# A graph, attention and expert layer on one core: work regrouped on GpSimd and VectorE, gate logits of 20 tiles moved off TensorE, 13 products added in a wait

## The chip, the cores and the metric

The kernel runs on one core of one Trainium2 chip. A core has five engines with a queue of instructions each: TensorE (PE in the profile; matmuls, with the loading of weights shown apart as PEld), VectorE (DVE), ScalarE (ACT), GpSimd (POOL) and SyncE (SP, which here only starts transfers). Engines wait for one another through semaphores alone. The metric is the device time of one execution in microseconds; less is better.

## The reference

Inputs are 3125 nodes with 256 features `x`, 53125 edges (`src`, `dst`, `edge_weight`) and the weights. All is float32. Cut to what matters:

```python
xn = layernorm(x)
# graph part: A is the weighted adjacency, A[src, dst] += edge_weight
h  = A @ xn                                   # 3125 x 256
S0 = softmax((A @ h) @ W0.T + b0)             # 128 wide
S1 = softmax((A @ S0) @ W1.T + b1)            # 128 wide
gnn = tanh([S0, S1] + h)
# attention part, linear: k and v are layer-normed per head of 64
kv  = einsum('bhsd,bhse->bhde', k, v) / S
mix = (q @ kv) @ wo.T + bo
x1 = x + gnn + mix
# expert part: 8 experts, each takes at most C = 489 of its tokens, in order
g = layernorm(x1)
logits = g @ gate_w + gate_b                  # 3125 x 8
idx, prb = argmax and max of softmax(logits)
pos  = running count of earlier tokens with the same idx
y = (relu(g @ w1[idx] + b1[idx]) @ w2[idx] + b2[idx]) * prb   if pos < C else 0
out = x1 + y
```

## The kernel before, in words

The nodes are cut into 25 tiles of 128. Everything on each engine is a list written out by hand; there is no planner. What sets the order is the order of each engine's list and the semaphores between them.

**First stage, a loop over `it`.** The dense adjacency is built in 157 units of up to four 128x128 blocks. In iteration `it` VectorE makes the one-hot matrices of unit `it-2` (`hots`, lines 990 to 999, three 128x512 operations), TensorE multiplies them (`build`, lines 1412 and 1414, unit `it-3`), ScalarE copies the result from PSUM (`evac`, line 706) and stores five units at a time to DRAM, and TensorE multiplies the unit by the layer-normed rows (`apply`, line 1429, unit `it-4`), which sums a strip of four node tiles in PSUM. `hots(u)` waits until `build(u-3)` is done. A strip has 25 units. At its end ScalarE and VectorE each copy one half of the sum to SBUF (`strip_out`; VectorE's at lines 1003 to 1006). TensorE may not start the next strip before both copies are done (semaphores `s_hevA`, `s_hevD`). VectorE's copy stands in the iteration in which it makes the one-hots of the unit five after the strip's last. `hidden_node` then turns the sums, tile by tile, and multiplies them by W0.

For `it` up to 30 the loop also sorts the edges (`spread`, `slot`, `ranks`, `slots`), computes layer norms and the key and value sums. `prepare(g)` unpacks a group of edges; `scales(g)` finishes the layer norm's factors, on which the first rows of ScalarE wait. At iteration 25 VectorE checks whether an edge has found no place (lines 1092 and 1093), and TensorE sums that and the gate weights (lines 1474 and 1475); the flag `rounds` decides on a fallback that these inputs don't take. At iteration 31 `kv_tail` (lines 1028 to 1040) finishes the key/value matrix on VectorE in 26 small operations, each waiting for the one before (`link`). TensorE turns it into the 256x256 matrix `M` at iterations 34 and 36. From iteration 40 every fourth one has a `mix(m)` on TensorE (line 1454), the attention output of tile `m`, which VectorE adds to the rows `X1` (line 1016). GpSimd adds the output bias `bo` to `X1` before that, all 25 tiles one after the other as soon as the layer norms are done (line 583).

**Graph layers.** SyncE loads the adjacency from DRAM in chunks of five units into a ring of five slots (line 515). `strip(l, k)` on TensorE (line 1576) is 25 products of 128x512, each two matmuls in the profile. Other work of TensorE is put in behind given products of a strip by the dictionary `inserts`. The second layer (`l == 1`) has eight strips: five of four tiles (0 to 19), then tiles 20-21, 22-23 and 24. With each goes this chain for the strip before: TensorE `turns` (line 1592), VectorE `biased` (1177, 1179), ScalarE the exponentials, VectorE `summed` (1184, 1186), ScalarE the tanh, VectorE `finished` (1193), `moments` and `root` (layer norm by Newton steps), `normal` (1246), which writes the normed rows `XN`.

**Gate.** TensorE turns the rows of `X1` (`gate_turn`, line 1335), ScalarE copies them (`xtout`, line 777), TensorE multiplies them by the gate weights (`logits`, line 1612, 16 matmuls for four tiles), and VectorE applies the factor and the bias and takes the maximum (`chosen`, lines 1223 to 1242). TensorE counts the tokens of each expert (`counts`), VectorE makes the row numbers (`slotted`), and GpSimd scatters the rows to DRAM by expert. TensorE waits for `counts(k)` of a strip, and so for `chosen(k)`, in the middle of the second strip after it. The loop on VectorE for strip `k` is `chosen(k-2)`, `biased(k-1)` and so on to `root(k-1)`, `slotted(k-2)`, `prob(k-2)`, `normal(k-1)`.

**Experts.** When the last row numbers are there, TensorE waits for the first expert's tokens (loaded back from DRAM), turns them and runs eight experts, `up` (line 1671) and `down` (line 1682).

Of the kernel before, what the change touches and what calls it, by code (L numbers as in the profile page):

```python
# [9 lines left out]
I32 = mybir.dt.int32  # L10
# [4 lines left out]
N = 3125  # L15
# [47 lines left out]
NGT = len(GATES)  # L63
SPLIT = 25
# [33 lines left out]
MIX_AT = {40 + 4 * _m: _m for _m in range(NT)}  # L98
T1_AT, M_AT = 34, 36
# [8 lines left out]
def graph_program(nc, a, out):  # L108
    ctx = ExitStack()
    with ctx:  # L110
# [150 lines left out]
        mv = gate[:, 843:893].rearrange("p (t a) -> p t a", a=2)  # L261
        iota_e = sb("iota_e", [P, NE])
# [21 lines left out]
        TURN = (2, 7)  # L284
        XTB = 3
# [82 lines left out]
        s_gturn = sem("s_gturn")  # L368
        s_xtb = sem("s_xtb")
# [48 lines left out]
        def _(sp):  # L418
# [80 lines left out]
            for l in (0, 1):  # L499
                for q in range(NC):  # L500
# [41 lines left out]
        def _(gp):  # L542
# [35 lines left out]

            gp.wait_ge(s_w, 16 * NWL)
# [5 lines left out]
            gp.wait_ge(s_m, 1)  # L585
            gp.memset(blank, 0.0).then_inc(s_blank, 1)
            gp.wait_ge(s_blank, 1)
            gp.memset(blank[:, ROW - 1:ROW].bitcast(I32), NOWHERE).then_inc(s_zero, 1)
# [42 lines left out]
        def _(act):  # L631
# [138 lines left out]
            def xtout(k):  # L770
                g = gate_of(k)
                act.wait_ge(s_gturn, k + 1)
                ge(act, s_lg, g - 1)
# [60 lines left out]
        def _(dve):  # L834
# [178 lines left out]
            def mixed(m):  # L1013
                dve.wait_ge(s_mixp, m + 1)
                dve.wait_ge(s_bo, m + 1)
                v.tensor_tensor(X1[:, m, :], X1[:, m, :], ps[:, MIXB, 0:D], ALU.add).then_inc(s_mrd, 1)

            def kv_tail():
                dve.wait_ge(s_kvt, NT)
                dve.wait_ge(s_vtot, 1)  # L1020
                for c in range(2):
                    sv = ps[:, PROD, c * P:(c + 1) * P].rearrange("p (h d) -> p h d", d=HD)
                    g_v = gvb[:, 0, :].unsqueeze(1).to_broadcast([P, 2, HD])
                    b_v = gvb[:, 1, :].unsqueeze(1).to_broadcast([P, 2, HD])
                    t = sq[:, 0:P].rearrange("p (h d) -> p h d", d=HD)
                    u = sq[:, P:2 * P].rearrange("p (h d) -> p h d", d=HD)
                    k2 = kvp[:, c, :].rearrange("p (h d) -> p h d", d=HD)
                    link(v.tensor_tensor(k2, ps[:, KVACC, c * (P + 1):c * (P + 1) + P].rearrange("p (h d) -> p h d", d=HD), g_v, ALU.mult))
                    link(v.tensor_copy(kvc[:, c:c + 1], ps[:, KVACC, c * (P + 1) + P:(c + 1) * (P + 1)]))
                    link(v.tensor_scalar(t, b_v, kvc[:, c:c + 1], None, ALU.mult))  # L1030
                    link(v.tensor_tensor(k2, k2, t, ALU.add))
                    link(v.tensor_scalar(k2, k2, cols[:, 1:2], None, ALU.mult))
                    link(v.tensor_tensor(t, sv, g_v, ALU.mult))
                    link(v.tensor_scalar(u, b_v, float(N), None, ALU.mult))
                    link(v.tensor_tensor(t, t, u, ALU.add))
                    link(v.tensor_scalar(t, t, cols[:, 2:3], None, ALU.mult))
                    link(v.tensor_tensor(k2, k2, t, ALU.add))
                    link(v.tensor_scalar(k2, k2, 1.0 / N, None, ALU.mult))
                    link(v.memset(kvp[0:HD, c, HD:P], 0.0))
                    link(v.memset(kvp[HD:P, c, 0:HD], 0.0))  # L1040
# [672 lines left out]
```

## Time and profile before

| what | us |
|---|---|
| median of the timed runs | 1217.53 |
| lowest and highest of 3 | 1216.27, 1220.08 |
| the profiled execution | 1206.22 |
| its span, first to last instruction | 1204.5 |
| TensorE busy | 1109.8 (92%) |
| VectorE busy | 704.4 (58%) |
| ScalarE busy | 320.1 (27%) |
| GpSimd busy | 157.4 (13%) |

The granted clock of TensorE was 0.964 of full speed on average. The first stage runs to 640 us, the first graph layer from 646 to 789 us, the second to 943 us, the experts from 964 us on. The page has shares of time; a share says nothing of where an engine's work could be missed, so the rows below are of stretches and of single instructions. A row of the time order has the start, the duration, the engine, the line, the operation with its output and input, and in brackets how long the engine had been idle before it and whose end it then followed. Rows with a count are several instructions in one piece. A matmul of float32 shows as two instructions.

### The profile page before, as it was taken

What the parts mean: (1) busy time and instruction counts of PE and PEld (TensorE: products, weight loads), DVE (VectorE), ACT (ScalarE), POOL (GpSimd) and SP (SyncE); (2) the same over time, 40 slices, a digit from 0 to 9 for tenths busy, and PEclk for the clock granted to TensorE, in tenths of its full rate; (3) what the DMA queues carried; (4) which work ended last, traced back from release to release, by engine and by line L of the source; (5) the groups of instructions that cost most, each with busy time, mean ns of one, the idle gap of its engine ahead of it and who ended that gap; (6) DMA issues with size and microseconds to landing.
All of it is one profiled execution on the core that took longest, in us unless ns stands there. A gap on an engine that the chain in (4) does not pass through costs nothing.

```text
span 1204.5 us, 14083 instructions
## 1 busy us (share of the span) xinstructions
PE 1109.8 (92%) x4909; PEld 703.4 (58%) x4909; DVE 704.4 (58%) x1566; ACT 320.1 (27%) x1035; POOL 157.4 (13%) x202
## 2 busy tenths in 40 slices
PE   4789899789999999999997999999999399999995
PEld 2456566456666666666674444545558366666664
DVE  7999999977777777777750011114546424444443
ACT  3667777311211212212220111101112122222220
POOL 1112222530000000000000000000234601111111
PEclk8889989989999999999998999999999789999998
DMA  6110111112333333342228988787885553344410
GB/s 171 11 41 12 45 45 45 44 44 88 123 123 123 123 123 123 123 166 88 88 103 307 360 315 299 268 316 263 299 298 194 169 188 113 114 134 137 151 43 7
DMA packets 65861, 175.39 MB, mean 146 GB/s; under 512 B 16607, under 2 KB 49146, under 8 KB 53758
## 3 DMA queue, kind: packets, MB, share of 16 engines
q1 hardware_dynamic: 53950, 123.74, 30.0%
q10 hardware_dynamic: 7520, 42.68, 8.8%
q0 software_dynamic: 4320, 8.04, 1.8%
q8 instruction: 42, 0.69, 0.2%
q14 instruction: 29, 0.24, 0.1%
HBM read 113.82 MB, written 63.01 MB: 147 GB/s over the span
## 4 chain that ended last, share of the span: by engine, by line
PE 82%; DVE 10%; issue 3%; SPq 1%; ACT 1%; DMA 1%; POOL 1%; POOLq 0%; DVEq 0%; ACTq 0%
PE ps L1576 22%; PE ps L1429 19%; PE ps L1412 11%; PE ps L1682 9%; PE ps L1671 9%; PE ps L1335 2%; PE ps L1454 2%; PE ps L1396 2%; PE ps L1382 1%; DVE W L950 1%; PE ps L1431 1%; DVE RING L990 1%; PE ps L1612 1%; DVE RING L996 1%; DVE RY L946 1%
## 5 line engine op out<-in xcount | busy, mean ns | idle before, releaser
L1429 PE MATMUL ps<-RING,XX 128*128 128x512 f32 x600 | 285.6, 599 | 8.8 <-DVE W L1006 8.6
L1576 PE MATMUL ps<-RING,RY 128*128 128x512 f32 (+2 forms) x750 | 276.3, 526 | 6.7 <-issue 6.7
L1576 PEld LDWEIGHTS ps<-RING,RY 128*128 128x128 f32 x750 | 134.0, 192 | 132.0 <-issue 129.9
L1412 PEld LDWEIGHTS ps<-RING 128*128 128x128 f32 x1250 | 164.5, 194 | 47.8 <-issue 46.5
L706 ACT COPY RING<-ps 128x512 f32<-128x512 f32 (+1 forms) x157 | 91.6, 584 | 335.8 <-PE ps L1412 319.0
L1412 PE MATMUL ps<-RING 128*128 128x128 f32 x1250 | 171.6, 279 | 3.8 <-DVE RING L999 3.8
L1429 PEld LDWEIGHTS ps<-RING,XX 128*128 128x128 f32 x600 | 103.9, 193 | 82.3 <-issue 82.1
L990 DVE TENSOR_TENSOR RING<-iota_n,RY 128x512 f32<-128x512 f32 (+1 forms) x157 | 108.6, 692 | 67.3 <-PE ps L1412 63.2
L996 DVE TENSOR_TENSOR RING<-iota_n,RY 128x512 f32<-128x512 f32 (+1 forms) x157 | 110.2, 702 | 0.0
L603 POOL DMA_INDIRECT xbuf_dram<-XX,sidx x25 | 25.4, 1015 | 631.4 <-DVE sidx L1258 625.6
L999 DVE TENSOR_TENSOR RING<-RING,RY 128x512 f32<-128x512 f32 x132 | 91.6, 694 | 0.0
L1317 DVE SCALAR_TENSOR_TENSOR W<-ps,RING,W 128x256 f32<-128x256 f32 (+1 forms) x32 | 15.5, 484 | 122.0 <-PE ps L1682 121.1
L825 ACT ACTIVATE RY<-ps,b1T 128x489 f32<-128x489 f32 x64 | 42.8, 669 | 162.0 <-PE ps L1671 162.0
L1162 DVE TENSOR_REDUCE nmx<-ps 128x4 f32<-128x512 f32 (+1 forms) x7 | 4.4, 635 | 114.6 <-PE ps L1335 114.6
L626 POOL DMA_INDIRECT out<-W,RING x32 | 31.3, 978 | 201.9 <-DVE W L1324 198.8
L1682 PE MATMUL ps<-RING,RY 128*128 128x256 f32 (+1 forms) x256 | 56.3, 381 | 0.8 <-ACT RY L825 0.8
L1682 PE MATMUL ps<-XT,RY 128*128 128x256 f32 (+1 forms) x256 | 56.3, 381 | 0.0
L1671 PE MATMUL ps<-RING,XT 128*128 128x489 f32 x128 | 54.9, 588 | 0.7 <-ACT RING L818 0.7
L1396 PE MATMUL ps<-wkvT,XT 128*128 128x512 f32 x100 | 50.5, 630 | 4.2 <-ACT XT L669 4.2
L1671 PE MATMUL ps<-RING 128*128 128x489 f32 x128 | 53.1, 574 | 0.0
L1682 PEld LDWEIGHTS ps<-RING,RY 128*128 128x128 f32 (+1 forms) x256 | 47.2, 186 | 9.4 <-ACT RY L825 1.5
L1682 PEld LDWEIGHTS ps<-XT,RY 128*128 128x128 f32 (+1 forms) x256 | 47.2, 186 | 7.9
(244 smaller groups left out, 1234.3 us busy)
## 6 DMA issues: line engine op xcount, KB each, us to landing
RING<-adj_dram SPq DMA_DIRECT2D x62, 1280.0 KB, 6.2
adj_dram<-RING ACTq DMA_DIRECT2D x31, 1280.0 KB, 4.5
XT<-in_L_ffn_w SPq DMA_DIRECT2D x8, 1024.0 KB, 7.6
RING<-in_L_ffn_w SPq DMA_DIRECT2D x8, 1024.0 KB, 6.5
rbuf_dram<-W SPq DMA_DIRECT2D x8, 516.0 KB, 5.2
RING<-rbuf_dram SPq DMA_DIRECT2D x8, 516.0 KB, 3.8
xbuf_dram<-W SPq DMA_DIRECT2D x8, 512.0 KB, 3.3
RING<-xbuf_dram SPq DMA_DIRECT2D x8, 512.0 KB, 4.7
```

What stands on the lines that cost most here:

```text
L626: gp.indirect_dma_start(out[:, :], bass.IndirectOffsetOnAxis(ap=xbs[0:n, e % 2, c, 2 * D + 1:ROW].bitcast(I32), axis=0), ybs[0:n, e % 2, c ...
L706: nc.scalar.copy(RING[:, n % 2, u % 5 * 512:u % 5 * 512 + w], ps[:, u % 2, 0:w]).then_inc(s_bev, 1)
L825: nc.scalar.activation(hmT[:, f, 0:CAPX], ps[:, 2 + f % 3, 0:CAPX], ACT.Relu, bias=b1T[:, f, e:e + 1]).then_inc(s_hidv, 1)
L990: v.tensor_tensor(h[:, 0, 0:n, :], every, grid(0), ALU.is_equal).then_inc(s_eq, 1)
L996: last = v.tensor_tensor(h[:, 1, 0:n, :], every, grid(1), ALU.is_equal)
L999: last = v.tensor_tensor(h[:, 0, 0:n, :], h[:, 0, 0:n, :], grid(2), ALU.mult)
L1396: last = nc.tensor.matmul(ps[:, PROD, :], XT[:, c, m * P:(m + 1) * P], wkvT[:, c, :], start=(c == 0), stop=(c == 1))
L1412: last = nc.tensor.matmul(o[:, i * P:(i + 1) * P], h[:, 0, i, :], h[:, 1, i, :], start=True, stop=(j != s))
L1429: last = nc.tensor.matmul(ps[:, ACC + dd, :], w, at, start=(j == 0), stop=True, skip_group_check=True)
L1576: last = nc.tensor.matmul(o, (Y if l == 0 else S0)[:, j, :], RING[:, slot_of[g % 5], i * across + first:i * across + first + w], start=(j ...
L1671: last = nc.tensor.matmul(ps[:, 2 + f % 3, 0:CAPX], w1s[s][:, c, f * P:(f + 1) * P], xbT[:, s, c, 0:CAPX], start=(c == 0), stop=(c == 1))
L1682: last = nc.tensor.matmul(o, hmT[:, f, c * P:c * P + n], w2s[s][:, f, :], start=(f == 0), stop=(f == 7))
```

## The change

It has these parts.

- GpSimd's bias add of tile `j` waits for unit `36 + 4j` of the build, and the blank rows are written before the bias adds, not after them.
- VectorE's copy of a finished strip stands two iterations sooner (`u - 3` for `u - 5`).
- `kv_tail` becomes four pieces at iterations 33 to 36; the products behind it move to 37 and 39. The check on edges moves from iteration 25 to 60, and its sums to another PSUM bank.
- `scales(0)` stands before `prepare(0)`.
- The last three `mix` products and their adds move behind the loop, into banks of their own.
- `DOTS = NGT - 2 = 5`: for the five strips of four tiles TensorE's `gate_turn` and `logits` and ScalarE's `xtout` are left out. VectorE computes the logits from `XN` in `dots(k-1)`, behind `normal(k-1)`: 160 products with a sum, each linked to the next. The gate weights come broadcast to all partitions by a transfer of 2048 numbers each, started by SyncE behind the load of chunk 5 of the second layer.
- `WARM = 13` products of 128x512 whose result nobody reads stand on TensorE between the last `counts` and the wait for the first expert's tokens.

```diff
+WARM = 13
+DOTS = NGT - 2
-MIX_AT = {40 + 4 * _m: _m for _m in range(NT)}
-T1_AT, M_AT = 34, 36
+MIX_AT = {40 + 4 * _m: _m for _m in range(NT - 3)}
+KV_AT, T1_AT, M_AT, FOUND_AT = 33, 37, 39, 60
...
+        gwb = HB[:, 0:16, 0:H].rearrange("p t (f e) -> p t f e", e=NE)
+        junk = xtf[:, 6144:6400].rearrange("p (t f) -> p t f", t=16)
+        mix_bank = lambda m: MIXB if m < NT - 2 else ACC + m - (NT - 2)
...
+                    if g == NC + 5:
+                        sp.wait_ge(s_sum[0], 4)
+                        sp.dma_start(HB[:, 0:16, 0:H], a["L0_ffn_gate_w"].rearrange("f e -> (f e)").partition_broadcast(P).rearrange("p (t r) -> p t r", t=16)).then_inc(s_gwb, 16)
...
             for j in range(NT):
                 gp.wait_ge(s_xn, j + 1)
+                gp.wait_ge(s_bmm, 37 + 4 * j)
                 gp.tensor_tensor(X1[:, j, :], X1[:, j, :], bo_b[:, :], ALU.add).then_inc(s_bo, 1)
...
-                xtout(k - 1)
                 zout(1, k)
...
             variances(0)
+            scales(0)
             prepare(0)
-            scales(0)
...
-                if u - 5 in ends[:-1]:
-                    strip_out(strip_of(u - 5))
-                if it == NT:
+                if u - 3 in ends[:-1]:
+                    strip_out(strip_of(u - 3))
+                if it == FOUND_AT:
...
-                if it == 31:
-                    kv_tail()
+                if it in (KV_AT, KV_AT + 2):
+                    kv_scaled((it - KV_AT) // 2)
+                if it in (KV_AT + 1, KV_AT + 3):
+                    kv_summed((it - KV_AT) // 2)
...
             strip_out(NS - 1)
+            mixed(NT - 3)
             hn_out(NT - 1)
+            mixed(NT - 2)
+            mixed(NT - 1)
...
+                if k < DOTS:
+                    v.tensor_tensor(tb, tb, each(gate_b[:, :]), ALU.add).then_inc(s_lgr, 1)
+                else:
+                    dve.wait_ge(s_lg, 1 if k == DOTS else NZ - DOTS)
...
+            def dots(k):
+                dve.wait_ge(s_gwb, 16)
+                dve.wait_ge(s_xn2, k + 1)
+                for j in GATES[k]:
+                    for e in range(NE):
+                        link(v.scalar_tensor_tensor(out=junk, in0=XN[:, j, :].rearrange("p (t f) -> p t f", t=16), scalar=1.0, in1=gwb[:, :, :, e],
+                                                    op0=ALU.mult, op1=ALU.mult, accum_out=tb8[:, j, e:e + 1]))
...
                 normal(k - 1)
+                dots(k - 1)
...
+            mix(NT - 3)
             hidden_node(NT - 1)
+            mix(NT - 2)
+            mix(NT - 1)
...
                 if k >= 2:
-                    inserts[2] = [later(logits, k - 2)]
                     inserts[10] = [later(counts, k - 2)]
                 if k >= 1:
                     inserts[5] = [later(turns, 1, k - 1)]
-                    inserts[23] = [later(gate_turn, k - 1)]
                 strip(1, k, inserts)
...
+            for _ in range(WARM):
+                nc.tensor.matmul(ps[:, XTB + 1, :], ident[:, :], S0[:, 0:4, :], start=True, stop=True)
             pe.wait_ge(s_slot, NGT)
             rows_in(0, 0)
```

## Rows read from the trace of the kernel before

**Rows 1.** Busy us of PE, PEld, DVE, ACT, POOL by stretch; clock, DMA share, GB/s.
```profile
300.00:400.00 100.00, 99.93 (x479) 66.23 (x477) 73.78 (x130) 21.09 (x36) 0.00 (x0) 1.00 0.35 135
850.00:900.00 50.00, 50.00 (x170) 26.02 (x170) 23.11 (x101) 8.14 (x26) 15.93 (x16) 1.00 0.90 302
```

**Rows 2.** TensorE in time order, 240 to 265 us.
```profile
242.84 3.75 PE L1429 MATMUL ps<-RING,XX 128*128 128x512 f32 x4 [8.57 <-DVE W L1006]
...
247.82 1.88 PE L1429 MATMUL ps<-RING,XX 128*128 128x512 f32 x4
...
259.62 0.68 PE L1412 MATMUL ps<-RING 128*128 128x128 f32 x4 [3.81 <-DVE RING L999]
...
261.31 3.06 PE L1429 MATMUL ps<-RING,XX 128*128 128x512 f32 x4
```

**Rows 3.** GpSimd and VectorE in time order, 232 to 258 us.
```profile
232.57 19.75 POOL L583 TENSOR_TENSOR XX<-XX,bo_b 128x256 f32<-128x256 f32 x25
...
235.26 1.21 DVE L996 TENSOR_TENSOR RING<-iota_n,RY 128x512 f32<-128x512 f32 x1
...
242.02 0.68 DVE L1006 COPY W<-ps 128x512 f32<-128x512 f32 x1
248.09 0.29 DVE L1028 TENSOR_TENSOR W<-ps,gvb 128x128 f32<-128x128 f32 x1 [5.40 <-PE ps L1485]
...
257.13 0.69 DVE L990 TENSOR_TENSOR RING<-iota_n,RY 128x512 f32<-128x512 f32 x1
```

**Rows 4.** TensorE in time order: one mix product, and the first strip.
```profile
321.42 1.03 PE L1454 MATMUL ps<-W,XT 128*128 128x256 f32 x4
...
646.38 18.03 PE L1576 MATMUL ps<-RING,RY 128*128 128x512 f32 x38 [6.68 <-issue]
```

**Rows 5.** Second layer: TensorE, VectorE's waits (total, times, longest), VectorE.
```profile
829.36 1.04 PE L1335 MATMUL ps<-ident,XX 128*128 128x128 f32 x8
830.24 3.60 PE L1576 MATMUL ps<-RING,RY 128*128 128x512 f32 x8
833.67 1.85 PE L1612 MATMUL ps<-gate_w,XT 128*128 128x8 f32 x16
835.37 2.82 PE L1576 MATMUL ps<-RING,RY 128*128 128x512 f32 x6
...
DVE wkvT L1223 <- PE ps L1612: 35.2, 4, 9.8
...
839.12 0.69 DVE L1177 TENSOR_TENSOR W<-ps,gb_b 128x512 f32<-128x512 f32 x1 [1.03 <-PE ps L1592]
...
850.37 1.35 DVE L1246 TENSOR_SCALAR XX<-XX,wkvT 128x256 f32<-128x256 f32 x4
860.73 0.63 DVE L1223 SCALAR_TENSOR_TENSOR wkvT<-ps,wkvT,gate_b 128x8 f32<-128x8 f32 x4 [9.01 <-PE ps L1612]
...
864.30 0.69 DVE L1177 TENSOR_TENSOR W<-ps,gb_b 128x512 f32<-128x512 f32 x1 [1.03 <-PE ps L1592]
```

**Rows 6.** VectorE in time order: linked 256-column operations, and one with a sum read-out.
```profile
997.93 0.43 DVE L1321 SCALAR_TENSOR_TENSOR W<-W 105x256 f32<-105x256 f32 x1
998.39 0.42 DVE L1322 SCALAR_TENSOR_TENSOR W<-W,RING 105x256 f32<-105x256 f32 x1
...
221.63 1.13 DVE L1093 SCALAR_TENSOR_TENSOR HB<-HB 128x450 bf16<-128x450 f16 x1
222.69 0.08 DVE L1093 DVE_READ_ACCUMULATOR HB<-HB 128x1 f32 x1
```

**Rows 7.** Wait for the tokens: TensorE, a stretch, and two rows of the chain of waits.
```profile
964.28 1.94 PE L1335 MATMUL ps<-ident,RING 128*128 128x128 f32 x8 [13.42 <-DMA RING<-xbuf_dram]
...
966.00:968.00 2.00, 1.33 (x4) 0.63 (x3) 0.00 (x0) 0.58 (x1) 0.00 (x0) 0.50 0.04 12
...
966.89 15.03 PE ps L1671 x32
...
996.76 13.12 PE ps L1671 x32
```

More of the change, by code:

```diff
@@ L1019, in kv_tail, with kv_scaled @@
+            def kv_scaled(c):
                 dve.wait_ge(s_kvt, NT)
                 dve.wait_ge(s_vtot, 1)
[L1021 to L1040, printed above, removed]
@@ L1041, in kv_tail @@
-                v.engine_nop().then_inc(s_kvp, 1)
+                k2 = heads(kvp[:, c, :])
+                link(v.tensor_tensor(k2, heads(ps[:, KVACC, c * (P + 1):c * (P + 1) + P]), g_v, ALU.mult))
+                link(v.tensor_copy(kvc[:, c:c + 1], ps[:, KVACC, c * (P + 1) + P:(c + 1) * (P + 1)]))
+                link(v.tensor_scalar(kv_t, b_v, kvc[:, c:c + 1], None, ALU.mult))
+                link(v.tensor_tensor(k2, k2, kv_t, ALU.add))
+                link(v.tensor_scalar(k2, k2, cols[:, 1:2], None, ALU.mult))
@@ new lines, in kv_summed @@
+            def kv_summed(c):
+                k2 = heads(kvp[:, c, :])
+                link(v.tensor_tensor(kv_t, heads(ps[:, PROD, c * P:(c + 1) * P]), g_v, ALU.mult))
+                link(v.tensor_scalar(kv_u, b_v, float(N), None, ALU.mult))
+                link(v.tensor_tensor(kv_t, kv_t, kv_u, ALU.add))
+                link(v.tensor_scalar(kv_t, kv_t, cols[:, 2:3], None, ALU.mult))
+                link(v.tensor_tensor(k2, k2, kv_t, ALU.add))
+                link(v.tensor_scalar(k2, k2, 1.0 / N, None, ALU.mult))
+                v.memset(kvp[0:HD, c, HD:P], 0.0).then_inc(s_kvp, 1)
+                v.memset(kvp[HD:P, c, 0:HD], 0.0).then_inc(s_kvp, 1)
@@ L1220, in chosen @@
                 tb, tc = tb8[:, t, :], tc8[:, 0:n, :]
-                dve.wait_ge(s_lg, k + 1 if k < NGT - 1 else NZ)
-                for i, j in enumerate(GATES[k]):
-                    last = v.scalar_tensor_tensor(out=tb8[:, j, :], in0=ps[:, LGB, i * NE:(i + 1) * NE], scalar=nr[:, 1, j:j + 1], in1=gate_b[:, :],
-                                                  op0=ALU.mult, op1=ALU.add)
-                last.then_inc(s_lgr, 1)
+                if k < DOTS:
+                    v.tensor_tensor(tb, tb, each(gate_b[:, :]), ALU.add).then_inc(s_lgr, 1)
+                else:
+                    dve.wait_ge(s_lg, 1 if k == DOTS else NZ - DOTS)
+                    for i, j in enumerate(GATES[k]):
+                        last = v.scalar_tensor_tensor(out=tb8[:, j, :], in0=ps[:, LGB, i * NE:(i + 1) * NE], scalar=nr[:, 1, j:j + 1], in1=gate_b[:, :],
+                                                      op0=ALU.mult, op1=ALU.add)
+                    last.then_inc(s_lgr, 1)
                 dve.wait_ge(s_lgr, k + 1)
@@ L1451, in mix @@
                 pe.wait_ge(s_mv, 1)
-                ge(pe, s_mrd, m)
+                if m < NT - 2:
+                    ge(pe, s_mrd, m)
                 for c in range(2):
-                    last = nc.tensor.matmul(ps[:, MIXB, 0:D], XT[:, c, m * P:(m + 1) * P], M[:, c, :], start=(c == 0), stop=(c == 1))
+                    last = nc.tensor.matmul(ps[:, mix_bank(m), 0:D], XT[:, c, m * P:(m + 1) * P], M[:, c, :], start=(c == 0), stop=(c == 1))
                 last.then_inc(s_mixp, 1)
@@ L1644, in _ @@
                     inserts[5] = [later(turns, 1, k - 1)]
-                    inserts[23] = [later(gate_turn, k - 1)]
                 strip(1, k, inserts)
-            strip(1, ka, {1: [later(logits, ka - 2)], 3: [later(turns, 1, ka - 1)], 12: [later(counts, ka - 2)], 21: [later(gate_turn, ka - 1)]})
-            strip(1, kb, {3: [later(turns, 1, ka)], 4: [later(logits, ka - 1)], 14: [later(counts, ka - 1)], 22: [later(gate_turn, ka)]})
+            strip(1, ka, {3: [later(turns, 1, ka - 1)], 12: [later(counts, ka - 2)]})
+            strip(1, kb, {3: [later(turns, 1, ka)], 14: [later(counts, ka - 1)], 22: [later(gate_turn, ka)]})
             strip(1, kc, {4: [later(turns, 1, kb)], 5: [later(logits, ka)], 21: [later(counts, ka), later(gate_turn, kb)]})
```

43 lines of the change are left out of this document (23 added, 20 removed).

## The prediction, made before the run

> **What bounds the kernel now.** I read the page first (shares of engines, then the 40 slices), then the busy time by stretches, then TensorE's waits in each stretch, and last the engines' rows in time order where a wait or a dip stood. Between 300 and 400 us TensorE is busy 99.93 of 100 us with VectorE at 73.78; between 850 and 900 us, in the second graph layer, TensorE has 50.00 of 50 us and VectorE 23.11 [rows 1]. So TensorE's order of work sets the end, and time can come back only where it stops. It stops in four places.
>
> At 234 to 247 us a product of the apply step stands 8.57 us behind VectorE's copy on line 1006 and then runs four matmuls in 3.75 us, where the same four take 1.88 us elsewhere; at 259.62 it stands 3.81 us more, and the matmuls after that wait are slow again, 3.06 against 1.88 us [rows 2]. VectorE's rows say why: GpSimd runs all 25 bias adds in one block of 19.75 us from 232.57, the 128x512 compare on line 996 takes 1.21 us beside it, and the like one takes 0.69 us once it is over; the awaited copy comes at 242.02, behind the slowed compares. Then the key/value tail holds VectorE from 248.09 to 257.13, and that is the second wait [rows 3]. The third is the 6.68 us before the first strip [rows 4]; the fourth is the 13.42 us for the first expert's tokens, after which TensorE runs at a granted clock of 0.50, its lower level of 1.2 GHz [rows 7].
>
> **The change, part by part.** All sums are against the profiled execution, 1206.22 us with a span of 1204.5; the median of the timed runs is 1217.53, 11.3 us higher for the same program. I take the difference in the profile and add it to the median.
>
> *First stage (bias paced, copy two iterations sooner, tail in four pieces, edge check later).* The paced bias runs one add per four units, so at most one compare in a dozen is lengthened, by about 0.5 us (1.21 less 0.69), and VectorE has 26 us in 100 free. The copy now comes right behind the compares of its own iteration, so the 8.57 us go. The tail's 9.04 us become four pieces of some 2 us, one per iteration, in iterations where TensorE has some 2.6 us of apply and build and VectorE 1.8 to 2.4 us of compares; VectorE starts this with about one unit of lead and falls behind by 2 to 4 us over the four, so I expect the 3.81 us to go and keep 1.5 us of it as the upper bound of what returns. With the stops go the slow stretches behind them: 3.75-1.88 = 1.87, and around the second 3.06-1.88 = 1.18 plus about 0.8 on the build matmuls in front of it. Sum: 8.57 + 3.81 + 1.87 + 2.0 = 16.3 us off. Bounds: 19 (the compares no longer slowed give a little more) and 5 us (half of the copy's wait stays, the tail's wait stays). Scales ahead of the first prepare, the blank rows ahead of the bias, the check at iteration 60: VectorE there waits for loads or has room, 0, within 1 us either way. The last pair of memsets, no longer waited for one by one: 0.
>
> *Three mix products behind the loop.* One takes 1.03 us of TensorE [rows 4], three some 2.7 us. They leave the full part and come just before the 6.68 us in which nothing but the sequencer and transfers run. If that pause starts later by what they take, almost nothing comes back (0.4 us, the part that lies in the wait for the last copies); if it ends with the transfers ahead of it, 2.6 us. I take 1.5.
>
> *Gate logits of 20 tiles on VectorE.* Off TensorE in each of five strips: the eight transposes, 0.88 us from their start to the next (829.36 to 830.24), and the 16 small products, 1.70 us (833.67 to 835.37) [rows 5]; 5 x 2.58 = 12.9 us, with ScalarE's copies. On VectorE: 20 tiles x 8 experts = 160 linked operations over 256 columns with a sum read-out. The trace has no such one. The nearest without the read-out is line 1321, 0.43 us long and 0.46 us from its start to the next linked one's. The one operation with a read-out, line 1093, shows the read-out starting 1.06 us into its 1.13 us, so it adds little behind the operation, 0 to 0.08 us [rows 6]. I take 0.48 us: 76.8 us in all. The gate bias add replaces four operations (0.63 us) by one of some 0.2, 5 x 0.44 = 2.2 us less. So 74.6 us are added.
>
> What covers them? VectorE waited 35.2 us in four pieces for the logits from TensorE and 1.03 us in each of three strips for the next turned tiles [rows 5]: 38.3 us. (The strips repeat every 25.2 us, 839.12 to 864.30.) Nothing else on VectorE between the first bias add at 814 and the last slot is a wait for TensorE of any size; the rest is its own chain and ScalarE's answers inside it. Read as a period: VectorE's chain of a strip is 839.12 to 851.72, 12.6 us, and the choice 2.5 us before it (now 2.1), so 14.7; with 32 products, 15.4 us, it is 30.1 us. TensorE's strip falls from 25.2 to 22.6 us. VectorE becomes the bound of the second layer by 7.5 us a strip, the count products of a strip wait for the choice, and TensorE stands in front of them. The 12.9 us saved are then waits. The fifth batch of products follows the last full strip, where no idle time was, and is paid whole. Behind it TensorE restarts from a stop of about 20 us, at half clock, with the two short strips that VectorE needs next: 2 us more. Sum: 74.6 - 38.3 + 2 = 38.3 us later. Its bounds: 0.37 us an operation (the same rows with the tail of the write hidden) gives 38.3 - 160 x 0.11 = 20.7; 0.74 us (twice the time per column) gives 38.3 + 160 x 0.26 = 79.9.
>
> The load of the broadcast gate weights, 1 MB in 512-byte pieces, goes in behind a ring load on the same queue, 30 us before its reader and with four ring slots loaded ahead of TensorE: 0, up to 3 us if it delays a ring load past its use. Ring loads meet a TensorE that is slower than before, so they need no more bandwidth.
>
> A rule stands against this change and would make it worse than my sum. The Trainium skill, "Vector Engine (DVE) Microarchitecture Reference", section "Points that are easy to get wrong", says of this two-source form that two SBUF sources that are not bfloat16 halve its throughput, since no read port is left for the accumulator. The only operation of this trace with the read-out, line 1093, has a length that fits the rule and fits a GpSimd neighbour as well [rows 6]; by the rule the time would be that of rival C, 1277, in place of 1235.
>
> *13 unread products in the wait.* 26 matmuls of 0.43 us (eight of this size lie between 830.24 and 833.67 [rows 5]) are 11.2 us, plus about 1.8 us because they start at half clock and, after the stop at 234 us, one group of four matmuls (3.75 us) passed before the next ran at full length: 13.0, in a wait of 13.42 [rows 2, 7]. So they end as the tokens land, at full clock. What comes back is the slow stretch behind the tokens: eight transposes in 1.94 us against 1.04 in rows 5, and a first up stage of 15.03 us against 13.12 for the second expert's [rows 7]: 0.9 + 1.9 = 2.8 us. Bounds: 4 (gains also further on) and -9 (they run at half clock throughout, 22.3 us, and hold the tokens up 8.9).
>
> Sum: -16.3 - 1.5 + 38.3 - 2.8 = +17.7 us. On the median, 1217.5 + 17.7 = 1235.2.
>
> **The rivals.**
>
> A, faster: TensorE stays the bound in the second layer. VectorE was busy only 23.11 of 50 us there, and 9.01 us of a strip were idle; if a batch of 32 took no more than that plus what TensorE gives back, the 12.9 us would be kept: 1217.5 - 16.3 - 1.5 - 12.9 - 2.8 = 1184. It decides at 0.29 us an operation. Against it: a plain 128x256 operation already takes 0.43 us, and the operations are linked one by one.
>
> B, no change: the operation takes 0.37 us, the layer loses 20.7 us and the other parts give 20.6: 1217.6. Against it the linked step of 0.46 us in [rows 6].
>
> C, slower still: twice the time per column. Line 1093 took 1.13 us for 450 columns; less 0.16 us of fixed time that is 2.2 ns a column, about twice that of line 1321. For 256 columns this gives 0.71, linked 0.74 us, and 1235.2 + 41.6 = 1277. Against it: line 1093 ran beside a GpSimd operation, and such company costs a compare 0.5 us, which explains the length as well.
>
> D, the first stage gives little: the four pieces and the earlier copy put VectorE behind, the 8.57 us return as several short waits and only 5 us are won: 1217.5 - 5 - 1.5 + 38.3 - 2.8 = 1246.5. For it: VectorE is gapless from 213 to 242 us. Against it: it is so beside GpSimd's block and the check, which both go.
>
> **How the numbers follow.** The forecast's mechanism with 0.44 to 0.56 us an operation: 0.63, giving 1229 to 1248. D 0.10; C 0.12; A 0.07; B with its neighbourhood 0.08, of which half lies within 0.3% of the old median (about what a measurement tells from no change). Faster: A 0.07, and 0.03 from B. Same 0.05. Slower 0.85. For 8 in 10 the range leaves A, most of B and most of C out: 1222 to 1265.
>
> **What would show it.** First stage right: no wait of 8 us behind line 1006's copy, compares at 0.69 us throughout, the tail in pieces. Logits: 160 operations at about 0.48 us from start to start, the stretch between the first turned tiles of layer two and the last slot 38 us longer, TensorE idle some 7 us in each strip ahead of the counts, VectorE without gaps. Wait: 26 matmuls between counts and tokens, and the first expert's stage 2.8 us shorter. Wrong if the operation's step is under 0.4 us or above 0.6, or if TensorE's idle time in the second layer is under 15 us.

## Result and profile after

The changed kernel took 1260.87 us (median of four runs, 1259.61 to 1261.46) where the kernel before took 1217.25 (1216.27 to 1220.08) beside it: ratio 1.0353, 95% interval 1.0334 to 1.0372. That is 43.6 us slower, where 17.7 us had been forecast; it lies inside the range, near its upper end, and the sign was right. The profiled execution took 1260.74 us with a span of 1258.9 us; TensorE's mean granted clock fell from 0.964 to 0.948.

The first fence is busy time by stretches in the kernel after. The columns are those of [rows 1]: busy us of PE, PEld, DVE, ACT and POOL, then the granted clock, DMA share and GB/s.

```profile
300.00:400.00 100.00, 100.00 (x481) 66.44 (x480) 76.34 (x137) 20.56 (x36) 11.75 (x9) 1.00 0.32 124
850.00:900.00 50.00, 33.08 (x87) 15.12 (x85) 44.59 (x155) 3.09 (x11) 12.46 (x13) 0.87 0.69 244
```

In the full part of the first stage TensorE is as busy as before. In the second graph layer it was busy all of 50 us; now it has 33.08, and VectorE went from 23.11 to 44.59. The bound has changed engine there. TensorE's waits in the kernel after name the place (total, times, longest, us):

```profile
PE ps L1651 <- DVEq L1252: 69.0, 5, 24.3
```

Line 1651 is the first count product of a strip, line 1252 the choice of the expert on VectorE. These are the waits that the forecast described, at 7 us a strip; they are 8.56, 10.39, 11.35, 14.43 and 24.30 us. What makes them stands in VectorE's time order (start, duration, engine, line, operation):

```profile
809.25 0.62 DVE L1271 SCALAR_TENSOR_TENSOR XT<-XX,HB 128x256 f32<-128x256 f32 x1
809.80 0.08 DVE L1271 DVE_READ_ACCUMULATOR XT<-XX,HB 128x1 f32 x1
809.91 0.62 DVE L1271 SCALAR_TENSOR_TENSOR XT<-XX,HB 128x256 f32<-128x256 f32 x1
...
830.37 0.08 DVE L1271 DVE_READ_ACCUMULATOR XT<-XX,HB 128x1 f32 x1
830.49 0.19 DVE L1236 TENSOR_TENSOR wkvT<-wkvT,gate_b 128x32 f32<-128x32 f32 x1
```

One product takes 0.62 us and the next begins 0.66 us after it did; 32 of them fill the 21.2 us from 809.25 to 830.49. The read-out of the sum starts 0.55 us into the product and ends with it. The forecast had 0.48 us a step, and said itself that a step above 0.6 would make it wrong.

The first stage, in TensorE's time order: the two apply groups next to the place where the waits of [rows 2] stood, and the first strip of [rows 4].

```profile
244.42 1.88 PE L1455 MATMUL ps<-RING,XX 128*128 128x512 f32 x4
...
247.25 1.88 PE L1455 MATMUL ps<-RING,XX 128*128 128x512 f32 x4
...
628.60 31.24 PE L1605 MATMUL ps<-RING,RY 128*128 128x512 f32 x66 [4.22 <-issue]
```

Neither long wait is left, the groups of four run in 1.88 us, and the first strip begins at 628.60 against 646.38 [rows 4]: 17.8 us sooner, of which 2.46 is the shorter pause (4.22 for 6.68).

Last, the wait for the first expert's tokens:

```profile
1007.05 14.29 PE L1713 MATMUL ps<-RY,ident 128*128 128x512 f32 x26
1021.18 1.04 PE L1361 MATMUL ps<-ident,RING 128*128 128x128 f32 x8
```

The eight transposes, line 1361 here, take 1.04 us, not 1.94 [rows 7], and start right behind the 26 matmuls.

Put together from the profile, by the second layer's bias additions on VectorE (count, duration in ns, first and last start, us), before and after:

```profile
L1177 DVE TENSOR_TENSOR W<-ps,gb_b x8: 292/690/692, 814.2 to 943.3; 128x512 f32<-128x512 f32 x5, 128x256 f32<-128x256 f32 x2, 128x128 f32<-128x128 f32 x1
L1191 DVE TENSOR_TENSOR W<-ps,gb_b x8: 291/686/691, 797.6 to 999.8; 128x512 f32<-128x512 f32 x5, 128x256 f32<-128x256 f32 x2, 128x128 f32<-128x128 f32 x1
```

All before the first of them gives 16.6 us. The stretch from the first to the last is 202.2 us, before 129.1, so 73.1 us longer. The two spans differ by 54.4 us (1258.9 and 1204.5), though the timed runs differ by 43.6: the two profiles come from unlike sessions, which the runs below sort out.

### The profile page after: what moved, and what is told of

It is laid out like the page before. It is cut to its first block, busy times and chain, and to the rows that moved or that the text cites. A ratio compares the mean times of both kernels' runs of the same rounds, so it can differ in the third digit from the quotient of the medians.

```text
span 1258.9 us, 14204 instructions
## 1 busy us (share of the span) xinstructions
PE 1123.5 (89%) x4815; PEld 702.1 (56%) x4815; DVE 801.2 (64%) x1871; ACT 315.7 (25%) x1025; POOL 169.6 (13%) x202
## 4 chain that ended last, share of the span: by engine, by line
PE 73%; DVE 19%; issue 3%; ACT 3%; SPq 1%; POOL 1%; DMA 0%; POOLq 0%; DVEq 0%; ACTq 0%
PE ps L1455 19%; PE ps L1605 14%; PE ps L1438 11%; PE ps L1710 9%; PE ps L1699 8%; DVE XT L1271 8%; PE ps L1422 2%; PE ps L1481 2%; PE ps L1361 2%; PE ps L1408 2%; PE ps L1713 1%; DVE W L958 1%; PE ps L1457 1%; ACT W L772 1%; ACT W L688 1%
## 5 line engine op out<-in xcount | busy, mean ns | idle before, releaser
L1605 PE MATMUL ps<-RING,RY 128*128 128x512 f32 (+2 forms) x750 | 289.0, 546 | 4.2 <-issue 4.2
L1455 PE MATMUL ps<-RING,XX 128*128 128x512 f32 x600 | 282.7, 594 | 0.3 <-ACT RING L716 0.3
L1605 PEld LDWEIGHTS ps<-RING,RY 128*128 128x128 f32 x750 | 141.8, 202 | 140.5 <-issue 136.8
L998 DVE TENSOR_TENSOR RING<-iota_n,RY 128x512 f32<-128x512 f32 (+1 forms) x157 | 107.9, 688 | 42.1 <-PE ps L1438 38.9
L1004 DVE TENSOR_TENSOR RING<-iota_n,RY 128x512 f32<-128x512 f32 (+1 forms) x157 | 117.1, 746 | 0.0
L1271 DVE SCALAR_TENSOR_TENSOR XT<-XX,HB 128x256 f32<-128x256 f32 x160 | 99.3, 621 | 5.9
L598 POOL TENSOR_TENSOR XX<-XX,bo_b 128x256 f32<-128x256 f32 x25 | 29.4, 1175 | 255.0 <-PE ps L1438 254.9
```

Of the source, the lines that this page charges most:

```text
L998: v.tensor_tensor(h[:, 0, 0:n, :], every, grid(0), ALU.is_equal).then_inc(s_eq, 1)
L1004: last = v.tensor_tensor(h[:, 1, 0:n, :], every, grid(1), ALU.is_equal)
L1271: link(v.scalar_tensor_tensor(out=junk, in0=XN[:, j, :].rearrange("p (t f) -> p t f", t=16), scalar=1.0, in1=gwb[:, :, :, e], op0=ALU.mult ...
L1455: last = nc.tensor.matmul(ps[:, ACC + dd, :], w, at, start=(j == 0), stop=True, skip_group_check=True)
L1605: last = nc.tensor.matmul(o, (Y if l == 0 else S0)[:, j, :], RING[:, slot_of[g % 5], i * across + first:i * across + first + w], start=(j ...
```

## Experiments

Each kernel was timed beside the kernel before on the same chip. Chips differ: the kernel before took 1208.7 us on the first four runs' chip, 1206.9 on the next four's and 1218.2 on the last four's. So ratios are compared, not times.

**The kernel before once more.** Its profile had shown 1206.22 us while the timed runs had a median of 1217.5.

> The kernel before, unchanged, once more with a profile. Its first profiled execution took 1206.2 us and its timed ones 1216 to 1220, while the changed kernel's agree with its profile within 2 us. Theory 1: one execution in several falls 11 us short in the first stage, where VectorE, GpSimd and TensorE meet at 200 to 270 us; then this profile shows about 1217 us and the 11 us stand as longer waits before 300 us. Theory 2: profiling itself shortens this kernel; then the profile shows 1206 us again and the timed runs 1217.

It took 1208.0 us (1206.6 to 1209.6), profiled at 1206.56, with the same waits. Neither theory: a profiled execution and timed ones agree on one chip, so the 11 us between the two figures of the prediction lie between sessions. Later profiles show where. On the last four runs' chip, where the kernel before takes 1218 us, a kernel whose second layer is as before ("paced alone" below) has its bias additions at these times:

```profile
L1178 DVE TENSOR_TENSOR W<-ps,gb_b x8: 292/687/692, 809.9 to 949.9; 128x512 f32<-128x512 f32 x5, 128x256 f32<-128x256 f32 x2, 128x128 f32<-128x128 f32 x1
```

That is 140.0 us (138.8 with the copy alone), where the two other chips give 129.1 to 129.3 for this layer. The difference lies in the last strips: TensorE stops there for 4.07 us, and a strip's 32 matmuls that take 3.82 us elsewhere take 6.17. What holds the engines up on that chip is not known. The forecast added a difference of profiles to a median from another session. This does touch it. Where the kernel before takes 1217 us, some 11 us of its second layer are, by this account, missing from the profile that the forecast was read from, and the changed kernel pays only 4 of them (shown with the adjacent numbers below).

**All gate logits back on TensorE**, the rest of the change kept.

```diff
-DOTS = NGT - 2
+DOTS = 0
...
-                dots(k - 1)
```

> The changed kernel with the gate logits of all tiles on TensorE again (transposes, ScalarE's copies, 16 small products a strip, no broadcast load, no products on VectorE); all other parts stay. Theory: the first stage gives 17.8 us (first strip at 628.6 against 646.4 in the profiles) and the 13 products about 2.8, so it is 20 us faster than the kernel before in the profiles: 1186 us in the profile; timed between 1186 (if the 11 us between profile and timed runs of the kernel before lie in what the change removes) and 1197. Rival: the other parts gain less than that, over 1205, and the logits are not the whole of the loss.

Ratio 0.9838 (0.9814 to 0.9863), 1187.8 us: faster than both kernels. Without the products on VectorE the rest of the change gives 19.6 us by the ratio and 20.8 by the medians; the forecast had 16.3 + 1.5 + 2.8 = 20.6.

**The same without the 13 unread products** (WARM = 0 in place of 13).

> The same without the 13 unread products. Theory: 2.8 us slower than with them, since the first expert's transposes and first up stage run at half clock again (1.94 and 15.0 us). Rival: the products hold the tokens' transposes up or the clock is back anyway, and it is equal within 1 us or faster.

Ratio 0.9857 (0.984 to 0.9875), 1190.4 us: 2.6 us more by the medians, 3.3 by the spans, though the two intervals overlap. TensorE's time order, first with and then without them:

```profile
933.57 13.06 PE L1709 MATMUL ps<-RY,ident 128*128 128x512 f32 x26
947.57 1.07 PE L1356 MATMUL ps<-ident,RING 128*128 128x128 f32 x8 [0.94 <-DMA RING<-xbuf_dram]
```

```profile
948.06 1.94 PE L1356 MATMUL ps<-ident,RING 128*128 128x128 f32 x8 [13.93 <-DMA RING<-xbuf_dram]
```

The 26 matmuls take the forecast's 13.0 us and fit the wait; behind them the transposes take 1.07 us, and 1.94 without them. The theory's 2.8 us held.

**The product by itself.** The changed kernel with four more operations in each of the first eleven tiles, whose results nothing reads. They vary three things: the stride of the second operand, the read-out of the sum, the width. The list is given in words, not as the code has it.

```diff
+forms = [stt(x, gate weights 8 numbers apart, read-out), stt(x, adjacent 16 x 16, read-out),
+         stt(x, adjacent 256, read-out), the first without read-out, the third without read-out,
+         the first with 128 columns, the third with 128, with 64, with 128 without read-out,
+         tensor_tensor adjacent, tensor_tensor 8 apart]
```

> The changed kernel; behind the eight products of each of the tiles 0 to 10 four more of one form a tile, whose sum goes to a spare column, so the result stays. Forms: 0 as in the change (second operand with a stride of 8 numbers, sum read out), 1 inner stride of 1, 2 flat 256 columns, 3 as 0 without the read-out, 4 flat without it, 5 and 6 as 0 and 2 with 128 columns, 7 flat with 64, 8 flat 128 without read-out, 9 and 10 a plain product of two tensors, flat and as 0. As 0 is 0.62 us long, step 0.66. Theory F (a fixed price of the read-out): without it 0.43, and 128 and 64 columns with it 0.13 and 0.20 us shorter than 256, strides without effect. Rival S (the stride): forms 1 and 2 at 0.43, forms 3 and 10 at 0.62. Rival R (the sum slows each column, as the rule of the skill has it): form 2 at 0.62, without it 0.43, and 128 columns with it at 0.62 less 128 x 1.8 ns = 0.39.

VectorE's time order, the last product of the first form and the first two of the second, then one row each of others; line 1274 holds the additional operations:

```profile
815.34 0.62 DVE L1274 SCALAR_TENSOR_TENSOR XT<-XX,HB 128x256 f32<-128x256 f32 x1
...
821.33 0.42 DVE L1274 SCALAR_TENSOR_TENSOR XT<-XX,HB 128x256 f32<-128x256 f32 x1
821.68 0.08 DVE L1274 DVE_READ_ACCUMULATOR XT<-XX,HB 128x1 f32 x1
821.79 0.42 DVE L1274 SCALAR_TENSOR_TENSOR XT<-XX,HB 128x256 f32<-128x256 f32 x1
...
835.63 2.58 DVE L1274 SCALAR_TENSOR_TENSOR XT<-XX,HB 128x256 f32<-128x256 f32 x4
...
858.41 1.81 DVE L1274 SCALAR_TENSOR_TENSOR XT<-XX 128x256 f32<-128x256 f32 x4
...
865.60 0.39 DVE L1274 SCALAR_TENSOR_TENSOR XT<-XX,HB 128x128 f32<-128x128 f32 x1
...
872.62 0.29 DVE L1274 SCALAR_TENSOR_TENSOR XT<-XX 128x128 f32<-128x128 f32 x1
```

With adjacent columns the product takes 0.42 us and a step of 0.46 to 0.47; the row at 858.41 is four without the read-out, 1.81 us, the same step. The row at 835.63 is the strided form four times without the read-out: 2.58 us, steps of 0.65, against 0.66 with it. From 128 to 256 columns the adjacent form grows by 0.13 us (1.04 ns a column) and the strided one by 0.23 (1.80 ns). So the second operand's distance of 8 numbers, 32 bytes, is what makes the product long: rival S held. The read-out costs nothing that can be seen, and the prediction's rival C, twice the time per column for any two such sources, is not there.

**The product read from adjacent numbers, in the whole kernel.** ScalarE lays the broadcast gate weights out by expert once, in eight copies.

```diff
-link(v.scalar_tensor_tensor(out=junk, in0=XN[:, j, :]..., scalar=1.0, in1=gwb[:, :, :, e], ...
+link(v.scalar_tensor_tensor(out=junk, in0=XN[:, j, :]..., scalar=1.0, in1=HB[:, 2 * e:2 * e + 2, 0:H], ...
+            for e in range(NE):
+                last = nc.scalar.copy(HB[:, 2 * e:2 * e + 2, 0:H], xtf[:, 4096:6144].rearrange("p (t f e) -> p e t f", t=2, e=NE)[:, e])
```

> The changed kernel as it is, beside the three others of this job, so that each can be set against it on one chip. Both theories: 1.0353 times the kernel before, about 1251 us where that one takes 1208; products on VectorE in steps of 0.66 us, TensorE's five waits ahead of the counts about 69 us in sum.

> The changed kernel, with the gate weights laid out once by ScalarE so that each product reads both operands without a stride. Theory S (the stride of the second operand makes the product 0.62 us instead of 0.42): the 160 products' step falls from 0.66 to 0.47 us, the stretch from the first bias column to the last index shrinks by 160 x 0.19 = 30 us, and the kernel takes about 31 us less than the changed one (1.010 of the kernel before, 1220 us), still slower than with all gate logits on TensorE (1188), since 160 x 0.47 = 75 us on VectorE are still covered only in part. Rival P (the place on VectorE and the lower clock cost it, not the length of one product): the steps shrink and the end comes less than 10 us sooner. Rival L (the eight copies on ScalarE come late and hold the first strip's products): VectorE waits for them, 5 us or more in one wait.

The changed kernel: ratio 1.0407 (1.039 to 1.0425), 1256.5 us. With adjacent operands: 1.0135 (1.0118 to 1.0152), 1223.6 us, 32.9 us less. The product's line in that kernel, with min, median and max ns, TensorE's wait, and the bias additions in the changed kernel on this chip and in this one:

```profile
L1275 DVE SCALAR_TENSOR_TENSOR XT<-XX,HB x160: 424/424/428, 807.6 to 941.2; 128x256 f32<-128x256 f32 x160
```

```profile
PE ps L1655 <- DVEq L1256: 41.7, 5, 17.6
```

```profile
L1191 DVE TENSOR_TENSOR W<-ps,gb_b x8: 291/686/691, 797.4 to 995.6; 128x512 f32<-128x512 f32 x5, 128x256 f32<-128x256 f32 x2, 128x128 f32<-128x128 f32 x1
L1195 DVE TENSOR_TENSOR W<-ps,gb_b x8: 292/686/691, 796.0 to 961.4; 128x512 f32<-128x512 f32 x5, 128x256 f32<-128x256 f32 x2, 128x128 f32<-128x128 f32 x1
```

The wait falls from 69.8 to 41.7 us, and the stretch between the first and the last bias addition is 165.4 us in place of 198.2. 160 steps of 0.19 us are 30.4 us. VectorE did not wait for the eight copies, so theory S held and rivals P and L did not. This kernel is what the forecast had priced: 16.7 us above the kernel before (0.0135 x 1208 = 16.3 by the ratio), against +17.7.

The changed kernel itself differs between the chips: 198.2 us for the stretch here, 202.2 in the result's profile. The two agree up to the end of the longest wait (979.30 and 979.41 us). The 4 us come behind 993 us, where TensorE shows three stops of 0.5 us and one of 0.3 that it doesn't have here, and its granted clock is down at 0.50 from 996 us on, where here it is still 0.84. So between a chip like this one and the result's, the kernel before loses 10.4 us (1206.9 and 1217.3) and the changed one 4.3 (1256.5 and 1260.9), which is the difference of the two ratios.

**Only two strips of six on VectorE**, with adjacent operands.

```diff
+ONV = (0, 2)
-                if k < DOTS:
+                if k in ONV:
...
+                    if k - 1 not in ONV:
+                        inserts[23] = [later(gate_turn, k - 1)]
```

> As the contiguous kernel, but only strips 0 and 2 of six have their products on VectorE, the others on TensorE. Theory V (VectorE has about 7.7 us to spare in a strip while TensorE is the bound; 38.3 us over five): two strips' products are 32 x 0.47 = 15 us each, 30 us in all, about what VectorE has to spare in the four strips from 0 to 3, so at best it ends with TensorE's relief of about 3 us a strip: 1182 to 1188 us, 0 to 6 less than with all of them on TensorE (0.983 of the kernel before). Rival W (the idle time of VectorE doesn't carry over from strip to strip, since the counts of a strip wait for its own choice): each of the two strips comes 15 - 7.7 = 7 us late, and it ends 8 to 14 us later than with all on TensorE, 0.990 to 0.995.

Ratio 0.9852 (0.9836 to 0.9868), the same as 0.9838 with none there, within the intervals. Two waits for the choice, 5.4 us in sum, take back what TensorE was relieved of (2 x 2.58 us). The loss of rival W isn't there, and of theory V only its lower edge, no gain.

**The first stage's edits in the kernel before**: bias additions paced (with the blank rows written ahead of them, as in the change), the copy two iterations sooner, and both.

```diff
+                gp.wait_ge(s_bmm, 37 + 4 * j)
```

```diff
-                if u - 5 in ends[:-1]:
-                    strip_out(strip_of(u - 5))
+                if u - 3 in ends[:-1]:
+                    strip_out(strip_of(u - 3))
```

> The kernel before, with two edits of the first stage alone: GpSimd's 20 bias additions paced, the blank rows set ahead of them, and a strip copied out of PSUM two iterations sooner. Theory F (these two carry the first stage's gain): TensorE's waits of 8.57 and 3.8 us go, the first strip of the second layer starts 12 to 15 us sooner, and the kernel takes 12 to 15 us less: 0.988 to 0.990. Rival K (the gain came from the tail of the projection in pieces and its later places): the two waits go, but TensorE waits in one place for the tail on VectorE instead, and less than 8 us is gained.

> The kernel before, with GpSimd's 20 bias additions paced one per four units instead of in one block, and nothing else of the first stage. Theory G (GpSimd's block lengthens VectorE's compares from 0.69 to 1.21 us, and that makes the copy late): with paced additions VectorE is not behind at 242 us, the wait of 8.57 us shrinks to under 3 us, and the kernel takes 6 to 10 us less (0.992 to 0.995). Rival Q (the copy of a strip out of PSUM stands too late in VectorE's own order, two iterations behind): the wait of TensorE stays at 5 us or more although the compares run in 0.7 us, and less than 4 us is gained.

> The kernel before, with the copy of a strip out of PSUM two iterations sooner, and nothing else. Theory Q (the copy's place makes the wait): the 8.57 us go although GpSimd still adds in one block and the compares still take 1.21 us; 8 to 11 us less, 0.991 to 0.993. Theory G (VectorE is behind because its compares are lengthened by GpSimd's block): the copy sooner only moves the wait to a compare, TensorE stands 3 us or more behind one, and less than 6 us is gained.

Paced alone: 0.9954 (0.994 to 0.9969), 5.9 us off. Copy alone: 0.9968 (0.9958 to 0.9977), 4.0 off. Both: 0.9899 (0.9881 to 0.9916), 11.1 us off, a little short of theory F's 12 to 15; the sum of the two is 9.9, which the intervals don't tell apart. The waits say more. TensorE's waits from 150 to 420 us, first paced alone, then the copy alone, then both:

```profile
PE ps L1430 <- DVE W L1007: 4.7, 1, 4.7
...
PE ps L1413 <- DVE RING L1000: 2.2, 1, 2.2
```

```profile
PE ps L1412 <- DVE RING L999: 10.0, 1, 10.0
...
PE ps L1429 <- DVE W L1006: 0.8, 1, 0.8
```

```profile
PE ps L1413 <- DVE RING L1000: 3.0, 1, 3.0
```

In the kernel before these two places cost 8.57 and 3.81 us [rows 2], 12.4 in sum; now 6.9, 10.8 and 3.0. Pacing nearly halves the first wait and no more: the compares take 0.67 us from 236 us on, but the copy keeps its late place, and until 235 us one compare in each iteration still takes 1.17 us beside GpSimd's layer-norm products. The sooner copy removes that wait, but with GpSimd's block still beside it VectorE is as late as before, and the lateness comes out behind the key/value tail: 10.0 us where it was 3.81. So the copy alone did what theory G said of it, and with paced additions alone both theories were half right (5.9 us gained, 4.7 us of wait left). With both, 3.0 us of the tail's wait stay; in the kernels that have the tail in pieces as well there is no wait at this place. With all edits of the change's first stage the first strip starts between 627.1 and 629.4 us, with these two alone at 636.0. The last 7 us or so belong to the tail in pieces, the later check, the scales and the mix products together and were not split.

**The last mix products in one bank** (in the kernel with all logits on TensorE).

```diff
-        mix_bank = lambda m: MIXB if m < NT - 2 else ACC + m - (NT - 2)
+        mix_bank = lambda m: MIXB
```

> The changed kernel with all gate logits on TensorE (0.9838 of the kernel before), in which the last two mix products go to the same PSUM bank as the others, each behind the addition that reads the one ahead of it. Theory T (behind the loop TensorE waits for transfers anyway, so the banks of their own give little): the pause ahead of the second stage's first strip grows by up to 2 us and that strip starts 0 to 1.5 us later; 0.984 to 0.986. Rival U (each product waits for VectorE's addition, about 1.2 us a time, on the path): it starts 2.4 us or more later, 0.986 or more.

Ratio 0.9826 (0.9806 to 0.9847): no difference from 0.9838. In the profiles the pause ahead of the first strip is 5.24 us, against 4.60, and one product waits 0.61 us for VectorE's addition. The strip starts 3.6 us later (631.99 and 628.37), but 2.0 us of that are there before the loop's last apply matmuls (620.07 and 618.11), where this edit has done nothing yet. So by the profiles the two banks are worth at most 1.7 us, about theory T's limit of 1.5, and by the times nothing measurable.

**Which distance costs.** As the product by itself, 128 columns, four operations each; the list again in words.

```diff
+forms = [second operand 1, 2, 4, 8, 16 numbers apart, first operand 8, both 8, output 2,
+         copy from 1, 8, 16 apart]
```

> The changed kernel, with four more two-source products or copies over 128 columns in each of the first eleven tiles, whose results nothing reads, to be read by their own lengths: second operand with a distance of 1, 2, 4, 8 and 16 numbers between columns, first operand with 8, both with 8, output with 2, and a plain copy with a distance of 1, 8 and 16. On record so far: 0.29 us at a distance of 1 and 0.39 us at 8, for 128 columns. Theory S1 (what costs is a distance of 32 bytes and more): 0.29 us up to a distance of 4, 0.39 us at 8 and at 16. Rival S2 (any distance but 1 costs the same): 0.39 us from 2 on. Rival S3 (the cost grows with the distance): 16 is longer than 8 by 0.05 us or more. If either operand costs, the first operand at 8 gives 0.39 us too, and both give 0.39 to 0.5 us; plain copies show whether it hangs on two sources.

Four of each in one row, in time order: distances 1, 2, 4, 8, 16, the first operand at 8, both at 8, the output at 2:

```profile
815.16 1.27 DVE L1274 SCALAR_TENSOR_TENSOR XT<-XX,HB 128x128 f32<-128x128 f32 x4
821.81 1.27 DVE L1274 SCALAR_TENSOR_TENSOR XT<-XX,HB 128x128 f32<-128x128 f32 x4
828.41 1.64 DVE L1274 SCALAR_TENSOR_TENSOR XT<-XX,HB 128x128 f32<-128x128 f32 x4
835.38 1.66 DVE L1274 SCALAR_TENSOR_TENSOR XT<-XX,HB 128x128 f32<-128x128 f32 x4
...
857.24 1.61 DVE L1274 SCALAR_TENSOR_TENSOR XT<-XX,HB 128x128 f32<-128x128 f32 x4
864.21 1.63 DVE L1274 SCALAR_TENSOR_TENSOR XT<-HB,XX 128x128 f32<-128x128 f32 x4
871.17 1.65 DVE L1274 SCALAR_TENSOR_TENSOR XT<-HB 128x128 f32<-128x128 f32 x4
878.14 1.27 DVE L1274 SCALAR_TENSOR_TENSOR XT<-XX,HB 128x128 f32<-128x128 f32 x4
```

None of the three theories: a distance of 2 is free, 4 and more cost the same 0.09 us on 128 columns (0.38 in place of 0.29 us). It is either operand, and both together cost no more than one. A plain copy goes from 0.226 to 0.275 us at 8 and 0.267 at 16, less than a product does.

## Why the prediction was right in kind and short in size

**Gate products on VectorE: the term that failed.** The mechanism came as put: 160 operations, VectorE without gaps, TensorE in front of the counts in all five strips, its 12.9 us saved turned into waits. The term was 38.3 us. It measured 69.1 on a chip where the kernel before takes as long as in the forecast's profile (198.2 less 129.1), 30.8 us too much. (The 73.1 us of the result's profile have 4 us of that chip in them.) What was wrong is the one duration in it, 0.48 us a step, taken from [rows 6]. That row is of the same instruction and width, but its operands are adjacent, and the change reads its second one 8 numbers apart: 0.66 us. The shape that a row prints says nothing of distances; the diff does (gwb ends in "(f e)" and is indexed by e). 160 x (0.66 - 0.48) = 28.8 of the 30.8 us. Adjacent operands gave 32.9 us back (160 x 0.19 = 30.4), and they leave the stretch at 165.4 us, 36.3 longer than before, for the forecast's 38.3. So the step for adjacent operands (0.47), VectorE's cover (38.3 us) and the 2 us for the half clock hold together as a sum; they were not measured one by one.

**Its bounds and rival C.** The upper bound, 0.74 us a step, held the true value. That the time fell inside the range was also luck with the chip: by the ratio of the second chip, 1.0407, the forecast's 1217.5 would have become 1267, above the range's 1265. And the mechanism given for that bound, from "Points that are easy to get wrong" in the Trainium skill's "Vector Engine (DVE) Microarchitecture Reference", isn't what acted: an adjacent product with read-out took 0.42 us, and so did one without. The prediction's own evidence for it, 1.13 us on line 1093, was GpSimd's doing: in the kernel after, the same instruction stands where GpSimd is idle (line 1102) and takes 0.63 us for its 450 columns.

```profile
323.79 0.63 DVE L1102 SCALAR_TENSOR_TENSOR HB<-HB 128x450 bf16<-128x450 f16 x1
```

The section "Measured stream behaviour on trn2" of the same page of the Trainium skill gives 1.73 ns a column where one source hops 4 KiB at every element and 1.054 where all are contiguous, and says that small non-adjacent steps cost more than large ones. This case shows 1.80 against 1.04 at a step of 32 bytes. An estimate from the page's two figures, 256 x 0.68 = 0.17 us more a product, would have moved the forecast by 28 us, to 1263. It was at hand and went unused.

**First stage.** Forecast 16.3 us and a first strip 17.8 us sooner with the mix products; measured 17.8 us, and 16.6 by the start of the second layer's bias additions. Rival D (only 5 us) fell. The forecast was right to take both edits: pacing alone gave 5.9 us, the copy alone 4.0, both 11.1. It had kept 1.5 us of the second wait as an upper bound of what returns; with the tail in pieces none of it did.

**Mix tail.** Forecast 1.5 us; the pause is 2.46 shorter. What it gives was not timed by itself, and its separate banks are worth nothing measurable.

**Unread products.** Forecast 2.8 us, measured 2.6 to 3.3 in the kernel with all logits on TensorE. In the changed kernel itself they take 14.29 us, 1.2 more, and end just as the transposes start. The granted clock (third number from the right below) is 0.50 there from 996 us on, 11 us before they begin; in the other kernel it is 1.00 until 928 us and at 0.50 to 0.52 from 930 us, 4 us before. Over the products it was:

```profile
996.00:1000.00 4.00, 3.44 (x15) 3.16 (x16) 0.91 (x5) 0.85 (x2) 1.53 (x2) 0.50 0.14 11
...
1008.00:1012.00 4.00, 4.00 (x6) 1.69 (x5) 1.06 (x8) 0.00 (x0) 1.95 (x3) 0.50 0.28 110
1012.00:1020.00 8.00, 8.00 (x19) 3.48 (x18) 0.00 (x0) 0.00 (x0) 6.48 (x6) 0.95 0.39 108
```

It is 0.50 (the level of 1.2 GHz) in the first 4 us, with TensorE busy all through them, and 0.95 over the next 8.

**Rivals A and B** needed a step of 0.29 and 0.37 us. The best layout gives 0.46, so VectorE would be the bound with any of these forms, and two strips of six already only break even. Where the layer's other engine has 7.7 us to spare in a strip, a batch of 15 to 21 us does not fit.

**What stays open.** Why the last strips of the second layer are 11 us longer on one chip than on two others is not known, and the kernel before has no profile on the result's chip: that its 1217 us there have the same place is argued from the equal time. Of the 30.8 us by which the stretch outgrew the forecast the steps leave 2 unexplained.

## To carry to other kernels

Before a duration is taken from a row of the same instruction and width, compare the distance between columns in both access patterns; in this float32 two-source operation on VectorE, 32 bytes made 1.80 ns a column out of 1.04, and laying the data out once (eight copies) won back 33 us. When work moves to an engine with idle time, compare its batch with the idle time in one period, 7.7 us here, not with the share of the stretch (23 of 50 us busy). Where an engine is late for two reasons, taking away one may only move the wait: measure them alone and together. Before a difference read in one profile is added to a time, see whether both come from the same chip: here one kernel took 1207 us on two and 1218 on another, and the changed kernel did not share most of that.

## What the runs showed of the hardware that was not expected

The cost of a distance between columns on VectorE starts between 8 and 16 bytes: 0.29 us for 128 columns at distances 1 and 2, 0.38 to 0.39 at 4, 8 and 16. One such operand and two cost the same (0.382 and 0.387 us). The Trainium skill's "Advanced Engine Details and Errata", section "SBUF Cachelines", speaks of 16-byte lines that need at least two accesses each for full rate; these runs agree with it. The Trainium skill's "Vector Engine (DVE) Microarchitecture Reference", section "Measured stream behaviour on trn2", asks for runs of at least two adjacent words, which would make a distance of 2 costly, which it wasn't. The read-out of a sum (0.08 us) lies inside the operation: steps with it and without it were equal, 0.46 to 0.47 us adjacent and 0.65 to 0.66 strided.
